# Products over 192 features as 128 and 64, fusion and gates in one program, sub-experts in one stage

## The reference, cut to what matters

```python
# layers 0 and 1: routed experts, 8 experts, hidden 768, best two for each token
logits = xn @ gate_w;  top = top_k(logits, 2);  gates = softmax(top)
y = sum over the two experts of gate * (act(xn @ w1[e] + b1[e]) @ w2[e] + b2[e])   # gelu in 0, silu without biases in 1
# layer 2, attention: linear attention (elu features) and local attention (window 64), fused by a gate
gate = sigmoid(relu(concat(lin_out, win_out, xn) @ W_g1 + b_g1) @ W_g2 + b_g2)
out = (gate * lin_out + (1 - gate) * win_out) @ W_out + b_out + residual
# layer 2, feed forward: 8 groups of 64 small experts (16 -> 32 -> 16), best four of each group
z = x @ P;  scores = z . C;  w = softmax(top_k(scores, 4))
comb = sum_k w_k * (gelu(z @ W1[k] + b1[k]) @ W2[k] + b2[k])
out = gelu(comb @ G1 + g1b) @ G2 + g2b
# layer 3, feed forward: each of 16 experts chooses its 204 best tokens, hidden 768, and a shared expert
y[ids] += score * ((silu(xg @ Wg.T) * (xg @ Wu.T)) @ Wd.T);  y += silu(x @ Ws_g.T) * (x @ Ws_u.T) @ Ws_d.T
```

## Time and profile before

| | us |
|---|---|
| median of three runs | 2238.52 |
| lowest, highest | 2233.54, 2240.09 |
| the profiled execution, its own time | 2217.4 |
| its span from first to last instruction | 2215.7 |
| PE busy | 1831.0 |
| DVE busy | 1252.6 |
| ACT busy | 892.4 |
| POOL busy | 356.4 |

### The profile page before, as it was taken

How to read it: one execution, slowest core, us unless ns; L and a number is a source line. 1 busy time by engine, 2 the same in 40 slices (tenths; PEclk the granted TensorE clock), 3 DMA queues, 4 the chain that set the end, 5 groups by cost and what they waited for, 6 DMA issues and landing times. The chain is left out here.

```text
span 2215.7 us, 40135 instructions
## 1 busy us (share of the span) xinstructions
PE 1831.0 (83%) x13693; PEld 1395.6 (63%) x13766; DVE 1252.6 (57%) x3619; ACT 892.4 (40%) x1938; POOL 356.4 (16%) x336
## 2 busy tenths in 40 slices
PE   5899789967775999588888559984999899749997
PEld 3678689956664999477655323332333688439997
DVE  1478822238997122478433658776788576782221
ACT  0245323314541121145332558866788355211211
POOL 0110121143211121551000000000000000223543
PEclk8999789978995899789898569986999999979998
DMA  5000356610003565110000850004000000404763
GB/s 192 1 1 0 123 138 164 164 31 16 9 25 117 146 159 132 54 37 6 0 1 0 131 102 1 1 1 78 11 1 0 22 0 0 119 24 112 180 157 60
DMA packets 68847, 139.39 MB, mean 63 GB/s; under 512 B 16803, under 2 KB 49635, under 8 KB 67683
## 3 DMA queue, kind: packets, MB, share of 16 engines
q1 hardware_dynamic: 50179, 121.03, 21.0%
q0 software_dynamic: 18528, 16.64, 3.6%
HBM read 115.37 MB, written 16.83 MB: 60 GB/s over the span
## 5 line engine op out<-in xcount | busy, mean ns | idle before, releaser
L2272 DVE TENSOR_TENSOR l2s_gated<-l2s_hidden,ps 128x408 f32<-128x408 f32 x512 | 262.7, 574 | 75.2 <-PE ps L2217 42.5
L2251 ACT ACTIVATE l2s_hidden<-ps,pack_l2f 128x408 f32<-128x408 f32 x512 | 265.9, 601 | 46.9 <-PE ps L2210 46.2
L1500 PE MATMUL ps<-l_xtT,l_up 96*128 96x128 f32 x1584 | 198.2, 284 | 3.4 <-DVE l_xtT L1761 3.4
L1500 PEld LDWEIGHTS ps<-l_xtT,l_up 96*128 96x128 f32 x1584 | 195.0, 200 | 4.7 <-DVE l_xtT L1761 4.7
L2210 PE MATMUL ps<-sub_zs,sub_up 128*128 x512 | 177.6, 348 | 20.9 <-ACTq L2246 19.0
L2217 PE MATMUL ps<-sub_gs,sub_spread 96*128 x512 | 178.1, 348 | 6.3 <-DVE l2s_gated L2272 6.0
L1511 PE MATMUL ps<-l_down,l_hidden 128*128 x792 | 140.1, 327 | 0.0
L2210 PEld LDWEIGHTS ps<-sub_zs,sub_up 128*128 128x128 bf16 x512 | 50.6, 99 | 136.4 <-ACT l2s_hidden L2251 79.3
L1511 PEld LDWEIGHTS ps<-l_down,l_hidden 128*128 128x128 f32 x792 | 128.2, 191 | 0.0
L2227 PE MATMUL ps<-l2s_gated,sub_down 128*32 128x408 f32 x1024 | 115.4, 523 | 1.2 <-DVE l2s_gated L2272 1.2
L125 PE MATMUL ps<-pack_const 128*128 128x512 bf16 x233 | 77.6, 452 | 41.2 <-PEq L159 16.2
(11 more groups left out here) (444 smaller groups left out, 3820.1 us busy)
## 6 DMA issues: line engine op xcount, KB each, us to landing
l_up<-in_l_up SPq DMA_DIRECT2D x66, 576.0 KB, 4.6
l3c_wg<-in_l_gate SPq DMA_DIRECT2D x16, 576.0 KB, 6.4
l3c_wu<-in_l_up SPq DMA_DIRECT2D x16, 576.0 KB, 8.0
l3c_wd<-in_l_down SPq DMA_DIRECT2D x16, 576.0 KB, 4.4
slots_out<-l_y SPq DMA_DIRECT2D x66, 96.0 KB
l_down<-in_l_down SPq DMA_DIRECT2D x8, 675.0 KB, 9.2
sub_gs<-l2g_g_parts SPq DMA_DIRECT2D x48, 102.0 KB, 3.1
l_down<-in_l_down SPq DMA_DIRECT2D x8, 576.0 KB, 7.0
```

The lines of the kernel that those rows point to most:

```text
L1500: last = pe.matmul(hid_bank(i, half)[:, t * 128:(t + 1) * 128], up[:, i % 3, c, n * 128:(n + 1) * 128], xtT[:, i % 2, c, :], start=(c == 0 ...
L2251: act.activation(hidden[:, n % kept, :], up_bank(n), ACT.Gelu_apprx_tanh, bias=w.at("b1")[:, s * MT + t:s * MT + t + 1]).then_inc(hid_read ...
L2272: dve.tensor_tensor(gated[:, n % (2 * RG), :], hidden[:, n % kept, :], gate_bank(n), ALU.mult)\
```

## The change

1. In the routed experts and in the last feed forward the 192 features are held as 128 and 64. An up product over 192 features is one product of 128 rows and one of 64 rows. The last 64 rows stand twice, in both halves of the partitions (the weights of two blocks side by side in one, the tokens turned twice), and the 64-row products of two blocks are given `tile_position` (0, 0) and (64, 0), writing two banks. The routing's turns and logits use 128 and 64 too.
2. Routing: DVE makes `passed` in one operation further ahead, POOL adds it up in four and copies it to `owner`. 24 fills follow the counts, 2 stand between the groups of `at_row` products, and 24 in place of 12 stand ahead of the tiles. ACT applies the stage's activation once to data that nobody reads.
3. `h += x` is done in the attention of layer 2, after its norm.
4. `gated_fusion` and both `sub_gates` become `fusion_and_gates`: six iterations in which the fusion's pieces and four steps of gates each stand in turn, then five more steps. The gate's parts, `sub_bias` and `sub_per_sum` all go to DRAM.
5. `sub_experts` runs once. It loads weights and parts in eight sets (two halves of eight samples, four sets of experts), has its loop written out as 256 pairs of tiles, one activation of 816 columns on each pair, and cuts each second product into two halves of 204 columns, between which other products stand. The output is at its end, with products of 64 rows.

The diff, cut to its core:

```diff
-                for c in range(C):
-                    last = pe.transpose(turned(i)[:, c * 128:(c + 1) * 128], xt[:, i % 3, c * K:(c + 1) * K], ident)
+                pe.transpose(turned(i)[:, 0:128], xt[:, i % 3, 0:WIDE], ident)
+                for twice in range(2):
+                    last = pe.matmul(turned(i)[REST * twice:REST * (twice + 1), 128:256], xt[:, i % 3, WIDE:D], ident,
+                                     start=True, stop=True, tile_position=(0, REST * twice))
                 last.then_inc(xtT_ps, 1)
...
-                for half in range(2):
-                    for t in range(3):
+                for t in range(3):
+                    for half in range(2):
                         n = 3 * half + t
-                        for c in range(C):
-                            last = pe.matmul(hid_bank(i, half)[:, t * 128:(t + 1) * 128],
-                                             up[:, i % 3, c, n * 128:(n + 1) * 128], xtT[:, i % 2, c, :],
-                                             start=(c == 0), stop=(c == C - 1))
-                    last.then_inc(hid_ps, 1)
+                        pe.matmul(hid_bank(i, half)[:, t * 128:(t + 1) * 128], up[:, i % 3, n * 128:(n + 1) * 128],
+                                  xtT[:, i % 2, 0, :], start=True, stop=False)
+                    for half in range(2):
+                        rows = slice(REST * half, REST * (half + 1))
+                        last = pe.matmul(hid_bank(i, half)[:, t * 128:(t + 1) * 128],
+                                         up[rows, i % 3, F + t * 128:F + (t + 1) * 128], xtT[rows, i % 2, 1, :],
+                                         start=False, stop=True, tile_position=(REST * half, 0))
+                        if t == 2:
+                            last.then_inc(hid_ps, 1)
...
-                for c in range(C):
-                    for a in range(2):
-                        last = pe.transpose(xgT_bank(e)[:, (c * 2 + a) * L:(c * 2 + a + 1) * L],
-                                            xg[:, e % RING, a, c * K:(c + 1) * K], ident[0:L, 0:L])
+                for a in range(2):
+                    pe.transpose(xgT_bank(e)[:, a * L:(a + 1) * L], xg[:, e % RING, a, 0:WIDE], ident[0:L, 0:L])
+                for a in range(2):
+                    for twice in range(2):
+                        last = pe.matmul(xgT_bank(e)[REST * twice:REST * (twice + 1), (2 + a) * L:(3 + a) * L],
+                                         xg[:, e % RING, a, WIDE:D], ident[0:L, 0:L],
+                                         start=True, stop=True, tile_position=(0, REST * twice))
                 last.then_inc(xgT_ps, 1)
...
-                for t in range(FM):
+                for t in range(0, FM, 2):
                     n = FM * e + t
-                    if n >= 4:
-                        pe.wait_ge(up_used, n - 3)
                     for u, wt in ((0, wg), (1, wu)):
-                        for c in range(C):
-                            last = pe.matmul(up_bank(n)[:, u * 2 * L:(u + 1) * 2 * L],
-                                             wt[:, e % RING, c, t * 128:(t + 1) * 128], xgT[:, e % 2, c, :],
-                                             start=(c == 0), stop=(c == C - 1))
-                    last.then_inc(up_ps, 1)
+                        for k in range(2):
+                            if n >= 4 and u == 0:
+                                pe.wait_ge(up_used, n + k - 3)
+                            pe.matmul(up_bank(n + k)[:, u * 2 * L:(u + 1) * 2 * L],
+                                      wt[:, e % RING, (t + k) * 128:(t + k + 1) * 128], xgT[:, e % 2, 0, :],
+                                      start=True, stop=False)
+                        for k in range(2):
+                            rows, at = slice(REST * k, REST * (k + 1)), F + t // 2 * 128
+                            last = pe.matmul(up_bank(n + k)[:, u * 2 * L:(u + 1) * 2 * L],
+                                             wt[rows, e % RING, at:at + 128], xgT[rows, e % 2, 1, :],
+                                             start=False, stop=True, tile_position=(REST * k, 0))
+                            if u:
+                                last.then_inc(up_ps, 1)
...
-                                         xT[:, c, (q * GB + b) * L:(q * GB + b + 1) * L],
-                                         w.at("gate", C)[:, c, :], start=(c == 0), stop=(c == C - 1))
+                                         xT[0:(WIDE, REST)[c], c, (q * GB + b) * L:(q * GB + b + 1) * L],
+                                         w.at("gate", 2)[0:(WIDE, REST)[c], c, :], start=(c == 0), stop=(c == 1))
...
             pe.matmul(ps[0:L, 1, 1, NE:2 * NE], const.at("earlier"), flat, start=True, stop=True)\
               .then_inc(count_ps, 1)
+            fill(pe, g, ps[:, 0, 0, :], 24)
 
             pe.wait_ge(named_ready, 1)
             for n in range(2 * B):
                 if n % 8 == 0:
+                    if n:
+                        fill(pe, g, ps[:, 0, 0, :], 2)
                     pe.wait_ge(at_row_ready, n // 8 + 1)
                 last = pe.matmul(ps[:, 1, 2, 0:2 * TILES], at_row[:, n, :],
                                  named[:, n, :, :].rearrange("p a i -> p (a i)"), start=(n == 0), stop=(n == 2 * B - 1))
             last.then_inc(tokens_ps, 1)
             pe.wait_ge(tokens_ready, 1)
-            fill(pe, g, ps[:, 0, 0, :], 12)
+            fill(pe, g, ps[:, 0, 0, :], 24)
             pe.wait_ge(owner_ready, 1)
             pe.wait_ge(down_loaded, 16 * E01)
             transposes(0)
...
+            for n, (into, other) in enumerate(((slice(0, 3), slice(3, 6)), (slice(0, 1), slice(6, 7)),
+                                               (slice(0, 1), slice(1, 2)), (slice(0, 1), slice(2, 3)))):
+                pool.wait_ge(passed_ready, n + 1)
+                pool.tensor_tensor(passed[:, into, :], passed[:, into, :], passed[:, other, :], ALU.add)\
+                    .then_inc(passed_ready, 1)
+            pool.wait_ge(passed_ready, 5)
+            pool.tensor_copy(owner[:, :], passed[:, 0, :]).then_inc(owner_ready, 1)
+
             pool.wait_ge(z_stored, 16)
...
+            dve.tensor_tensor(passed[:, :, :], iota[0:1, 0:TILES].unsqueeze(1).broadcast_to([1, E01 - 1, TILES]),
+                              tiles_of[1][0:1, 4:3 + E01].unsqueeze(2).broadcast_to([1, E01 - 1, TILES]), ALU.is_ge)\
+               .then_inc(passed_ready, 1)
...
+            act.activation(unread[:, :], gap[:, :], func)
...
+                if keep:
+                    steps.wait()
+                    for tile in pair(n):
+                        steps.done(dve.tensor_tensor(h[:, tile, :], h[:, tile, :], x[:, tile, :], ALU.add))
...
-def gated_fusion(nc, g):
...
+def fusion_and_gates(nc, g, dram):
...
+        def steps_of(q):
+            return [GB * (q - 2) + k if q >= 2 else -1 for k in range(GB)]
+
+        LAST = B + 5
...
             for q in range(G + 2):
+                at = steps_of(q)
                 if q < G:
                     lin_products(q)
-                if q >= 2:
-                    fused_transposes(q - 2)
-                    out_products(q - 2)
+                step(at[0])
                 if q < G:
                     lin_values(q)
                 if 1 <= q <= G:
                     mix_transposes(q - 1)
                     gate_hidden(q - 1)
+                step(at[1])
                 if q < G:
                     lin_scores(q)
                 if 1 <= q <= G:
                     gate_products(q - 1)
+                step(at[2])
                 if q < G:
                     lin_outputs(q)
+                if 1 <= q <= G:
+                    fused_transposes(q - 1)
+                step(at[3])
+                if 1 <= q <= G:
+                    out_products(q - 1)
+            for t in range(B, LAST):
+                step(t)
...
-            for base in (0, HALF):
-                sub_gates(nc, g, dram, sub, base)
-                sub_experts(nc, g, sub, base)
-        sub_output(nc, g, sub)
...
+    order = [(half, r, odd, t, pair) for half in range(2) for r in range(2) for odd in range(2)
+             for t in range(MT) for pair in range(2)]
+    pairs, per_sum_bank = len(order), len(order) // 2
...
+            for half in range(2):
+                for k in range(4):
+                    if not half:
+                        weights(k)
+                    parts(half, k)
+                    if not half and not k:
+                        sp.dma_start(comb[:, :, :, :, :], g["sub_bias"]).then_inc(sums_loaded, 16)
+                        sp.dma_start(per_sum[:, :, :, :, :], g["sub_per_sum"]).then_inc(sums_loaded, 16)
...
+            def second(n, part):
+                at_bank, cols = n // per_sum_bank, slice(part * NG // 2, (part + 1) * NG // 2)
+                if n % per_sum_bank == 0:
+                    if part:
+                        return
+                    cols = slice(0, NG)
+                    if at_bank:
```

(18 more changed lines are left out.)

1181 lines of the change are left out of this document (589 added, 592 removed).

## The result

| | us |
|---|---|
| the changed kernel, median of 4 | 2294.43 (2293.7 to 2301.66) |
| the kernel before, median of 4, same series | 2236.45 (2233.54 to 2240.09) |
| ratio | 1.0275 [1.0253, 1.0297] |
| the same two in a later series | 2278.37 (4 runs) and 2211.5 (7 runs) |
| ratio there | 1.0303 [1.0275, 1.0332] |

The forecast was slower, 2317, range 2190 to 2360. The change costs 58 us in the first series and 67 in the later one; 78 were forecast.

What follows compares the result with a forecast made beforehand. TensorE was taken as the bound (busy 1831.0 of 2215.7 us), except in fusion and gates. Terms +60, +11, +9, -8, +3, +3 gave +78: 2295 on the profile, 2317 beside the median 2238.5; range 2190 to 2360.

Steps and rivals of the forecast that it cites:

- Parts 1 and 2: Up products of 66 routed tiles and 16 chosen experts: shape changes cost about 0.195 and 0.185 us each; +60 and +11.
- Rival A: Routed tiles and chosen experts: a shape change costs only the bare 0.095 us; +7 and -9, total 2244; chance 0.10.
- B (nothing): Routed tiles, chosen experts and column halves: 64-row groups change shape at no cost; -43, -30, -24, total 2149; chance 0.12.
- Rival E: Routed tiles and chosen experts: the two row groups don't run side by side; +77, total 2394; chance 0.05.
- Part 3: Routing of both layers: +9 for logits, transposes and their tail, -8 for fills ahead of the tiles.
- the term of -8: First two routed tiles of each layer: added fills hold TensorE's clock; -8 us for both layers, range -12 to +5.
- Routing's +9: Routing, both layers: logits and transposes alternating between 128 and 64 rows, with their tail on TensorE; +9 us, range 0 to 16.
- Part 4: Local attention: h += x, moved there from the fusion in 32 small pieces, may delay a pair; +3 us, range 0 to 6.
- Part 5: Fusion and gates in one program: DVE has the longest list and its waits stay; 285 us, bounds 200 to 320.
- C (215): Merged fusion and gates: closes its waits and runs near DVE's list, 215 in place of 285; total 2247; chance 0.16.
- D (320): Merged fusion and gates: runs at 320 us because TensorE's clock stays at 0.57; total 2352; chance 0.07.
- Part 6: Sub-experts in one stage: halved second products, four tiles in 2.58 us, 341 in all; output 14 for 19.8.

Runs made afterwards that it cites:

- grouped order: The changed kernel with 128-row products first, then 64-row ones, in routed tiles and chosen experts' block pairs: 2207.58 us, 0.9961 of the kernel before.
- the alternation: The changed kernel with each routed 128-row up product followed at once by its own 64-row product: 2428.6 us, one execution.
- no_fills: The changed kernel with the routing's fills as before (none after the counts or between groups, 12 ahead of the tiles): 2273.07 us, 1.028 of the kernel before.
- the second profile: The changed kernel profiled again, unaltered, in a later series: span 2275.9 us, local attention 188.8 us; median there 2278.37 us, 1.0303 of the kernel before.

## Why the prediction was right, step by step

*Parts 1 and 2* were right to the tenth: 5.77 us a tile (5.76 in the working), +11.4 for the experts. The step that carried them, 0.095 us until the next shape may start and the first weight load on top, was read from row groups of 32 and a column of 32; it holds for groups of 64, where both parts can be read in single records (0.205 in place of 0.112, then 0.207). The grouped order and the alternation test it from both sides, so it is shown: the price is per change and not per product. Rival A (0.095 alone) and B (nothing) would have given 4.97 and 4.21; both are refuted. Rival E too: in the changed kernel four records of 64 rows take 0.42, as two slots and a change do. The rule of the Trainium skill, "TensorEngine Tiling (Array Packing)", Key Properties, that a switch of the mode drains the engine, is borne out with a number to it; and what the same section says of tiles, that they load weights and multiply in parallel, holds for two groups of 64 rows (0.42 and not 0.64). The factor of up to two in its Theoretical Speedup shows in the 64-row products themselves (twelve records in 0.86 us with their change, in the grouped run, where twelve slots of 0.112 would be 1.34) and not in the tile: with the fewest changes, it still took 4.99 us against 4.87.

*Part 3*: the term of -8 came out at -11.2, and not for the reason given. The fills don't bring the first tiles to full clock; it rises without them, and they cost 5 us. Routing's +9 measured +5.8, the fills' 5 among them, so the 64-row forms of turns and logits and the moved table together cost next to nothing (no_fills: 1.1 us in the first layer, none in the second): I had priced them as if TensorE were the limit all along.

*Part 4*: +3 forecast, +1.8 against the kernel before, and 5.5 at most against the same kernel without the additions.

*Part 5*: the program takes 284.9 us from the first linear product (1130.5) to its last store (1415.4), where 285 was forecast; the loads take 21 and not 25. In the second profile, the program's body and the hole behind it, and SP's last store and first load:

```profile
1131.00:1415.00 284.00, 202.02 (x832) 128.44 (x830) 139.41 (x637) 131.02 (x344) 4.04 (x4) 0.75 0.10 28
1415.00:1431.00 16.00, 0.00 (x0) 0.00 (x0) 3.56 (x4) 2.34 (x2) 0.00 (x0) 0.50 0.81 148
```

```profile
1414.94 0.47 SPq L1148 DMA_DIRECT2D sub_per_sum<-l2b_per_sum  x1
1418.21 0.36 SPq L2223 DMA_DIRECT2D l2s_gated<-in_sub_spread  x1
```

DVE is busy for 139.4 of 284 us: the merging hides little, as forecast, and TensorE's clock stays at 0.75. Its waits (engine, line, what it waited for, in total, times, longest):

```profile
DVE l2b_best L1569 <- ACT x L1404: 57.8, 12, 12.2
DVE pack_l0a L1596 <- ACT l2b_gT L1440: 27.8, 16, 3.6
DVE l2b_lin_f L1478 <- ACT pack_l1a L1351: 17.2, 3, 8.5
DVE rows_z L1525 <- PE ps L1230: 11.7, 1, 11.7
```

The sum of the waits was right, their distribution in part. 57.8 us go to the scores, twelve times, and 34.6 of them in three waits of 11.7, 10.7 and 12.2, one in each iteration that has both `gate_hidden` and steps of gates. One of these on TensorE and DVE:

```profile
1263.83 1.53 PE L1222 MATMUL ps<-xT_all,pack_l2a 96*96 96x408 f32 x4
1265.19 0.34 PE L1282 MATMUL ps<-pack_const,x 102*96 102x102 f32 x2
1265.37 1.02 PE L1289 MATMUL ps<-pack_l2f,l2b_sT 128*102 128x512 f32 x2
1267.06 1.11 DVE L1569 MAX8 l2b_best<-x 102x8 f32<-102x64 f32 x8 [10.72 <-ACT x L1404]
```

L1222 is `gate_hidden`, whose 24 records run from 1254.8 to 1265.4; the turns (L1282) and scores (L1289) of the next step stand behind it. This is the wait that the working put at 7.5, and it is larger. The wait for the gate's products themselves (L1525) came once, 11.7, in the iteration without gates. The linear products cost 17.2 in all, near the 16 of the working, but as 8.5 and 6.5 in the iterations without gates, 2.3 in the first with them, and none in the next. By iterations: the first two without steps of gates 56 us for 63, the next three 177 for 170, the rest 52 for 52. Two misses of 7 cancel, so that the agreement to a tenth of a microsecond is luck, where the forecast within some us is not. Rivals C (215) and D (320) are refuted.

*Part 6*: 334.9 and not 341: four tiles take 2.56 and not 2.58, 2.6 us in all, and the start and the four sums cost less than the 11 I had added; the output as forecast.

*The whole*: the sum was 18 us too high: 3 from the first tiles, 3 from the routing, 2.5 from a stage that I held unchanged, 4 each from parts 5 and 6, one each from part 4 and the output. The profiled 2293.7 beside the forecast of 2295 on the profile's basis is luck: 19 us of it come with the late rise of the clock in the local attention. Against the medians the 21.1 added for the difference between profile and runs was sound in that series (2236) and would have been wrong in the later series (2211 to 2215).

## What to carry to other kernels

Count the changes of the array's shape in the order of issue, as separate terms of the sum: here 0.095 us plus a weight load each, which turned a saving of 0.56 us a tile into a loss of 0.9. Here the products of 64 rows paid only where they were issued in groups and each was long (204 columns: 7.6 us won in the last stage against 96 rows; 128: 0.12 a tile lost): compare the slots saved for each change, times the length of a slot, with the price of a change. And before a difference of two profiles is explained stage by stage, profile the same kernel a second time: a stage that both kernels share moved by 19 us here with no edit at all.

## What the runs showed that I had not expected

The local attention has two courses. TensorE's granted clock came to stay at full speed some 72 or some 134 us into the stage, with the same instructions, and the stage took 188.8 or 208.1 us. Fills that cost 5 us were of no use to the clock at the place where they stood, while four more fills in the kernel before were worth 6 (0.9972 [0.9954, 0.9989]). In strict alternation of shapes the clock stayed at half until 318.5 with TensorE busy for 15.06 of 16 us before, where the changed kernel has full clock from its first routed tile on, and 29 us went beyond the changes themselves.
